# Graph attention over image windows: the neighbour sums run over all 128 rows, with a shifted copy of transposed x

## The reference, cut to what matters

```python
alpha = _bn_relu(einsum('bchw,oc->bohw', x, wa), ...)      # 32 channels, the queries
sigma = _bn_relu(einsum('bchw,oc->bohw', x, ws), ...)      # 32 channels, the keys
att = einsum('bkn,bkm->bnm', af, sf)
att = softmax(where(adj, att, NEG), axis=2)                # adj: the 8 neighbours of a pixel
h_s = einsum('bnm,bcm->bcn', att, xf)
Gc = einsum('bcn,bdn->bcd', xf, xf)
catt = softmax(where(cadj, Gc, NEG), axis=2)               # cadj: the channels c-1 and c+1
h_p = einsum('bcd,bdn->bcn', catt, xf)
out = (1.0 - gama) * x + gama * elu(h_s + h_p)
```

## Time and profile before

| what | value |
|---|---|
| median of 3 runs | 502.03 us (498.39 to 506.97) |
| the profiled execution, its own time | 500.11 us |
| its span | 498.0 us |
| mean granted TensorE clock | 0.982 |
| busy: TensorE, weight loads, ScalarE, VectorE, GpSimd | 93%, 70%, 69%, 68%, 59% |

### The profile page before, as it was taken

One profiled execution on the slowest core, in us unless ns is written; L12 is line 12 of the kernel. 1 busy time (PEld: TensorE's weight loads), 2 busy tenths in 40 slices (PEclk: granted clock), 3 DMA queues, 4 the chain that ended last, 5 costly groups with the idle time before them and its releaser, 6 DMA issues.

```text
span 498.0 us, 17890 instructions
## 1 busy us (share of the span) xinstructions
PE 461.8 (93%) x7172; PEld 350.4 (70%) x7172; DVE 339.3 (68%) x693; ACT 341.7 (69%) x980; POOL 295.2 (59%) x198
## 2 busy tenths in 40 slices
PE   1679999999999999999999999999999999999993
PEld 1346777768777786877767786877778687777783
DVE  6016676677767676766768677686767777686895
ACT  3336867677786777677776767787677776867571
POOL 8000566566756676567657656775666667665770
PEclk9998999999999999999999999999999999999985
DMA  7956667677776777676677767777677777644123
GB/s 224 264 137 166 190 206 241 194 217 225 224 226 211 236 209 239 206 238 210 206 228 215 243 203 226 222 228 224 217 218 231 219 224 226 197 156 143 65 107 128
DMA packets 55746, 102.01 MB, mean 205 GB/s; under 512 B 6256, under 2 KB 6640, under 8 KB 55664
## 3 DMA queue, kind: packets, MB, share of 16 engines
q1 hardware_dynamic: 55664, 100.88, 65.6%
HBM read 34.00 MB, written 33.55 MB: 136 GB/s over the span
## 4 chain that ended last, share of the span: by engine, by line
PE 84%; ACT 8%; DVE 3%; issue 3%; DMA 1%; SPq 0%; DVEq 0%; ACTq 0%
PE z L475 31%; PE gb L475 20%; PE xp L485 14%; PE score L475 12%; PE et L562 6%; ACT elu L302 2%; ACT key L263 2%; ACT upper L253 2%; PE gb L508 1%; ACT upper L267 1%; DVE elu L384 1%; DMA wt<-w_dram 1%; DVE z L379 1%; DVE probs_t L372 0%; DVE bn L424 0%
## 5 line engine op out<-in xcount | busy, mean ns | idle before, releaser
L228 POOL TENSOR_SCALAR elu<-elu,vec,mix 128x1024 f32<-128x1024 f32 x61 | 72.8, 1193 | 178.6 <-DVE elu L384 178.6
L475 PE MATMUL z<-probs_t,upper 64*128 64x128 f32 (+1 forms) x2304 | 173.2, 284 | 4.5 <-DVE probs_t L372 2.4
L475 PEld LDWEIGHTS z<-probs_t,upper 64*128 64x128 f32 x2304 | 155.2, 190 | 28.4 <-issue 24.1
L232 POOL TENSOR_TENSOR blend<-elu,blend 128x1024 f32<-128x1024 f32 x61 | 144.0, 2361 | 9.4 <-POOL elu L228 0.5
L302 ACT ACTIVATE elu<-z 128x512 f32<-128x512 f32 x128 | 69.7, 600 | 70.8 <-PE z L475 70.8
L384 DVE SCALAR_TENSOR_TENSOR elu<-elu,z 128x512 f32<-128x512 f32 x128 | 82.0, 682 | 35.4 <-ACT elu L302 35.4
L278 ACT ACTIVATE score<-score,neg_max 128x128 f32<-128x128 f32 x256 | 86.5, 338 | 25.1 <-DVE neg_max L355 25.1
L253 ACT ACTIVATE upper<-xp 128x512 f32<-128x512 f32 x128 | 76.8, 600 | 39.2 <-PE xp L485 39.2
L485 PE MATMUL xp<-const,x 128*128 128x128 f32 x512 | 87.2, 295 | 14.5 <-ACT upper L253 8.4
L379 DVE SCALAR_TENSOR_TENSOR z<-near,catt,z 128x512 f32<-128x512 f32 x128 | 90.4, 750 | 7.3 <-ACT z L293 6.6
L293 ACT ACTIVATE z<-x,catt 128x512 f32<-128x512 f32 x128 | 83.6, 695 | 2.4 <-DVE elu L384 2.4
(11 more groups left out here) (52 smaller groups left out, 244.1 us busy)
## 6 DMA issues: line engine op xcount, KB each, us to landing
x<-x_dram SPq DMA_DIRECT2D x64, 512.0 KB, 6.0
out_dram<-blend SPq DMA_DIRECT2D x61, 512.0 KB, 3.6
near<-x SPq DMA_DIRECT2D x128, 224.0 KB, 4.5
near<-x SPq DMA_DIRECT2D x128, 30.0 KB, 4.1
out_dram<-blend SPq DMA_DIRECT2D x6, 256.0 KB, 2.0
const<-constants_dram SPq DMA_DIRECT2D x1, 243.5 KB, 7.9
const<-constants_dram SPq DMA_DIRECT2D x1, 128.0 KB, 2.1
wt<-w_dram SPq DMA_DIRECT2D x1, 64.0 KB, 3.8
```

Source lines behind the costliest of these rows:

```text
L228: nc.gpsimd.tensor_scalar(elu[s % 2][:, :, :], elu[s % 2][:, :, :], vec[:, V_GAMA:V_GAMA + 1], mix[:, 1:2], ALU.mult, ALU.add).then_inc(ga ...
L232: nc.gpsimd.tensor_tensor(blend[s % BLENDS][:, :, :], elu[s % 2][:, :, :], blend[s % BLENDS][:, :, :], ALU.add).then_inc(blend_done, 1)
L475: return nc.tensor.matmul(o, l, r, start=start, stop=stop, skip_group_check=True, **kw)
```

## The change

The half-height products of z are replaced by products over all 128 partitions. A second copy of transposed x, `lower`, holds for each window v the lower half of group v on partitions 64 to 127 and the upper half of group v+1 on partitions 0 to 63. Two DMAs per step copy it from `upper`; the last group's upper half is written by ScalarE as before, now into `lower`. Then kind 0 of window v is one product with `upper[v]` and kind 1 is one with `lower[v]`, each of 64 columns. That is 4 windows by 2 kinds by 2 banks, 16 products for a step, in one phase.

With it go these edits. All z of step t-2 is summed once, near the end of the slot. `gram_band` part 2 moves behind the transposes of the probabilities, and part 3 behind z. `z_done` is raised once per bank, so `exp_z` of h waits for bank h alone. `near` shrinks from two whole images to five quarters, is built two slots ahead of its use in place of four, and is cleared by five smaller operations. The waits that named the old counts are rewritten.

```diff
-        near = [sb(f"near{j}", [P, HALF, N]) for j in range(2)]
-        upper = [sb(f"upper{j}", [P, GROUPS + 1, C]) for j in range(2)]
+        near = [sb(f"near{j}", [P, HALF, QN]) for j in range(NEAR_BUFS)]
+        upper = [sb(f"upper{j}", [P, GROUPS, C]) for j in range(2)]
+        lower = [sb(f"lower{j}", [P, GROUPS, C]) for j in range(2)]
...
-                    sp.wait_ge(near_in[(b - XBUFS) % 2][q], NEARS * ((b - XBUFS) // 2 + 1))
+                    sp.wait_ge(near_in[s % NEAR_BUFS], NEARS * (s // NEAR_BUFS + 1))
                 sp.dma_start(xs[b % XBUFS][:, :, cols(q)], x_img[b][:, :, q * QN:(q + 1) * QN])\
                     .then_inc(x_in[b % XBUFS][q], 16)
 
-            def build_near(b, q):
+            def build_near(s):
+                b, q = s // QUARTERS, s % QUARTERS
                 sp.wait_ge(x_in[b % XBUFS][q], 16 * (b // XBUFS + 1))
-                if b >= 2:
-                    sp.wait_ge(mix_done, 2 * ((b - 2) * QUARTERS + q) + 2)
-                j, signal = b % 2, near_in[b % 2][q]
+                if s >= NEAR_BUFS:
+                    sp.wait_ge(mix_done, 2 * (s - NEAR_BUFS) + 2)
+                to, signal = near[s % NEAR_BUFS], near_in[s % NEAR_BUFS]
                 xb = xs[b % XBUFS]
                 for lo, hi in ((0, SPREAD), (SPREAD, P - 1)):
-                    sp.dma_start(near[j][lo + 1:hi + 1, 0, q * QN:(q + 1) * QN], xb[lo:hi, 1, cols(q)]).then_inc(signal, 16)
-                    sp.dma_start(near[j][lo:hi, 1, q * QN:(q + 1) * QN], xb[lo + 1:hi + 1, 0, cols(q)]).then_inc(signal, 16)
+                    sp.dma_start(to[lo + 1:hi + 1, 0, :], xb[lo:hi, 1, cols(q)]).then_inc(signal, 16)
+                    sp.dma_start(to[lo:hi, 1, :], xb[lo + 1:hi + 1, 0, cols(q)]).then_inc(signal, 16)
+
+            def build_lower(s):
+                b, q = s // QUARTERS, s % QUARTERS
+                sp.wait_ge(xt_out, 2 * s + 2)
+                if b >= 2:
+                    sp.wait_ge(z_done, 2 * (s - 2 * QUARTERS) + 2)
+                j, g0 = b % 2, q * GQ
+                g1 = g0 + (q == 0)
+                sp.dma_start(lower[j][0:KEYS, g1 - 1:g0 + GQ - 1, :], upper[j][0:KEYS, g1:g0 + GQ, :])\
+                    .then_inc(lower_in[j][q], 16)
+                sp.dma_start(lower[j][KEYS:P, g0:g0 + GQ, :], upper[j][KEYS:P, g0:g0 + GQ, :])\
+                    .then_inc(lower_in[j][q], 16)
...
-            sp.wait_ge(near_zero, 2)
+            sp.wait_ge(near_zero, NEAR_BUFS)
             for t in slots:
                 b, q = t // QUARTERS, t % QUARTERS
+                if real(t + 3):
+                    build_lower(t + 3)
                 if b + 1 < B:
                     sp.wait_ge(xt_done, 2 * t + 2 * QUARTERS + 1)
                 if b + 2 < B:
                     load_x(b + 2, q)
-                if b + 1 < B:
-                    build_near(b + 1, q)
+                if real(t + 2):
+                    build_near(t + 2)
...
-                    act.wait_ge(z_done, (b - 1) * QUARTERS)
-                nc.scalar.activation(upper[b % 2][0:KEYS, GROUPS, :], gb[0:KEYS, EDGE:EDGE + C], ACT.Copy)\
+                    act.wait_ge(z_done, 2 * (b - 1) * QUARTERS)
+                nc.scalar.activation(lower[b % 2][0:KEYS, GROUPS - 1, :], gb[0:KEYS, EDGE:EDGE + C], ACT.Copy)\
...
-                act.wait_ge(z_done, s + 1)
+                act.wait_ge(z_done, 2 * s + h + 1)
...
-                    k = P if g < GROUPS else KEYS
+                    rows_t = upper[b % 2][:, g, :] if g < GROUPS else lower[b % 2][0:KEYS, GROUPS - 1, :]
                     for blk in range(P // HID):
                         mine, other = blk * HID, P + blk * HID - 1
-                        last = mm(gb[mine:mine + HID, 0:BAND], upper[b % 2][0:k, g, mine:mine + HID],
-                                  upper[b % 2][0:k, g, other:other + BAND], g == 0, g == GROUPS, tile_position=(0, mine))
+                        last = mm(gb[mine:mine + HID, 0:BAND], rows_t[:, mine:mine + HID], rows_t[:, other:other + BAND], g == 0, g == GROUPS,
+                                  tile_position=(0, mine))
...
-            def z_sums(s, phase):
-                b, q = s // QUARTERS, s % QUARTERS
-                if phase == 0:
-                    pe.wait_ge(pt_out, s + 1)
-                    pe.wait_ge(mix_done, 2 * s + 2)
-                else:
-                    pe.wait_ge(z_half, s + 1)
-                up, pt = upper[b % 2], probs_t[s % 2]
-
-                def add(row, h, g, lo, hi):
-                    return mm(z[s % 2][h][:, lo:hi], up[row:row + KEYS, GQ * q + g, h * P:(h + 1) * P],
-                              pt[row:row + KEYS, lo:hi], False, True, tile_position=(row, 0))
-
-                even, odd = phase, 1 - phase
-                add(0, even, 0, 0, KEYS)
-                for g in range(GQ):
-                    add(64, odd, g, g * WIN, (g + 1) * WIN)
-                    last = add(0, even, g + 1, g * WIN + KEYS, min((g + 1) * WIN + KEYS, QN))
-                last.then_inc(z_done if phase else z_half, 1)
+            def z_sums(s):
+                b, q = s // QUARTERS, s % QUARTERS
+                pe.wait_ge(pt_out, s + 1)
+                pe.wait_ge(mix_done, 2 * s + 2)
+                pe.wait_ge(lower_in[b % 2][q], 32 * (b // 2 + 1))
+                if q < QUARTERS - 1:
+                    pe.wait_ge(lower_in[b % 2][q + 1], 32 * (b // 2 + 1))
+                pt = probs_t[s % 2]
+                for h in range(HALF):
+                    for v in range(GQ):
+                        for c, rows_t in enumerate((upper[b % 2], lower[b % 2])):
+                            n0 = v * WIN + c * KEYS
+                            last = mm(z[s % 2][h][:, n0:n0 + KEYS], rows_t[:, GQ * q + v, h * P:(h + 1) * P],
+                                      pt[:, n0:n0 + KEYS], False, True)
+                    last.then_inc(z_done, 1)
...
-                if real(t - 2):
-                    z_sums(t - 2, 0)
-                if own:
-                    gram_band(b, 2)
                 if b + 1 < B:
                     transpose_x(b + 1, q, 1)
                 if real(t - 1):
                     transpose_probs(t - 1)
                 if own:
-                    gram_band(b, 3)
+                    gram_band(b, 2)
                 if q == 2 and 0 < b + 1 < B:
                     project_odd(b + 1)
                 if real(t - 2):
-                    z_sums(t - 2, 1)
+                    z_sums(t - 2)
+                if own:
+                    gram_band(b, 3)
                 if q == 1 and 0 < b + 1 < B:
                     project_query(b + 1)
                 if t == -1:
```

More of the change, by code:

```diff
@@ L29 @@
 NEARS = 4 * 16
+NEAR_BUFS = 5
 C_ID, C_DOWN = 0, P
@@ L104, in graph_attention @@
         x_in = [[sem(f"x_in{j}{q}") for q in range(QUARTERS)] for j in range(XBUFS)]
-        near_in = [[sem(f"near_in{j}{q}") for q in range(QUARTERS)] for j in range(2)]
+        near_in = [sem(f"near_in{j}") for j in range(NEAR_BUFS)]
+        lower_in = [[sem(f"lower_in{j}{q}") for q in range(QUARTERS)] for j in range(2)]
         stored = [sem(f"stored{i}") for i in range(BLENDS)]
@@ L138, in graph_attention @@
         mix_done = sem("mix_done")
-        z_half = sem("z_half")
         z_done = sem("z_done")
@@ L237, in _ @@
                 nc.gpsimd.memset(xs[j][:, :, W + N:N + 2 * W], 0.0).then_inc(pads_done, 1)
-            for j in range(2):
+            for j in range(NEAR_BUFS):
                 nc.gpsimd.memset(near[j][:, :, :], 0.0).then_inc(near_zero, 1)
@@ L251, in move_xt @@
                 if b >= 2:
-                    act.wait_ge(z_done, (b - 2) * QUARTERS + q + 1)
+                    act.wait_ge(z_done, 2 * ((b - 2) * QUARTERS + q) + 2)
                 nc.scalar.activation(upper[b % 2][:, g:g + 2, :], xp[:, :].rearrange("p (v c) -> p v c", v=2),
@@ L370, in move_probs @@
                 if s >= 2:
-                    dve.wait_ge(z_done, s - 1)
+                    dve.wait_ge(z_done, 2 * (s - 2) + 2)
                 nc.vector.tensor_copy(probs_t[s % 2][:, :], et[:, :]).then_inc(pt_out, 1)
@@ L375, in mix_channels @@
                 b, q = s // QUARTERS, s % QUARTERS
-                dve.wait_ge(near_in[b % 2][q], NEARS * (b // 2 + 1))
+                dve.wait_ge(near_in[s % NEAR_BUFS], NEARS * (s // NEAR_BUFS + 1))
                 dve.wait_ge(product_done, 2 * s + h + 1)
                 zh = z[s % 2][h]
-                nc.vector.scalar_tensor_tensor(zh[:, :], near[b % 2][:, h, q * QN:(q + 1) * QN], catt[:, h, h:h + 1],
+                nc.vector.scalar_tensor_tensor(zh[:, :], near[s % NEAR_BUFS][:, h, :], catt[:, h, h:h + 1],
                                                zh[:, :], ALU.mult, ALU.add).then_inc(mix_done, 1)
```

## The result

The kernel after takes 663.0 us in the median (654.6 to 663.9, 4 runs) against 504.5 us for the kernel before in the runs beside it: a ratio of 1.322, with a 95% interval of 1.302 to 1.342. The profiled execution spans 661.0 us, 163.0 more than before, and its mean granted TensorE clock is 0.833, where it was 0.982. I had forecast 578 us and a range of 560 to 612.

The account below looks back on a forecast made before the run. TensorE, busy for 93% of the span, was taken as the bound. Per image +4.20 + 0.10 + 0.95 - 0.40 = +4.85; sixteen images, less 0.95 for the first, give 76.7, plus 0.7 at the end, on 500.11: 578 us, range 560 to 612.

Parts of the forecast that it names:

- rival (a): TensorE's clock falls to 1.2 GHz at the open wait before the shift, 1.7 us each: 604 (0.10) or 686 us (0.09).
- my milder case: The clock falls about once per image, 1.7 us each, adding 27 us for 604 us in all; chance 0.10.
- the clock held through every image before: Argument against clock falls: in the trace before, the clock held in every image between first and last, 1.00 in one shown.
- z, four steps: z's 32 full-height loads set the pace at 0.111 us each: 3.55 us per step against 2.50, +4.20 per image.
- wait behind the band, scores included: Nothing hides VectorE's small operations ahead of the shift, and `normalise` delays the scores: +0.95 per image, between 0.8 and 1.2.
- wait in q 3: TensorE's 0.54 us wait for ScalarE before `project_even` shrinks as the first exponential starts earlier: -0.40 per image.
- seams: Costs where TensorE changes tile shape between groups, some vanishing, some dearer: +0.10 per image, between -0.2 and +0.4.
- another +0.7 for the half clock: At the end, the last z at half clock costs 2.3 more in place of 1.05, less 0.5 for the earlier exponential.
- Rival (b): In z, a full-height load waits for the matmul ahead: 0.166 us per product, 690 us in all; chance 0.05.
- Rival (c): z's full-height load is as short as a transpose's: 0.066 us per product, about 486 us, DMA engines nearly full; chance 0.07.
- The second part, the scores behind `normalise`: `normalise`, queued behind `gram_pick` on VectorE, releases the scores 1.70 us behind the band, TensorE being ready at 1.65.
- The copy, `near`, the queues: The two added transfers per step, the later `near` and the issues on SP's queue cost zero; waits on them are over when reached.

Follow-up runs that it names:

- run 3: Kernel after, with every product of z streaming 128 columns in place of 64 (sums not the reference's): 583.5 us, ratio 1.162.
- run 2: Kernel after, with four bfloat16 products of 512 columns, never read, put in the wait ahead of the shift: 571.4 us, ratio 1.135.
- run 5: Kernel before, with only TensorE's order changed to that of the kernel after, z keeping its half-height products: 554.6 us, ratio 1.090.
- Run 1: Kernel after, with part 3 of the band moved back in front of z: 572.1 us, ratio 1.129.
- run 4: Kernel after, with every product of z streaming 32 columns in place of 64, half the queries left out: 835.6 us, ratio 1.665.
- run 9: On top of run 2, same count of z's loads and matmuls, each over 64 rows, banks on the array's two halves, half the keys left out: 508.2 us.
- run 7: On top of run 2, the DMAs that build `lower` and the waits on them left out, both products reading `upper`: 571.3 us, ratio 1.128.
- run 8: Kernel after, with part 3 of the band back in front of z and every product of z streaming 128 columns: 553.5 us in two runs.

## Why the prediction was wrong

The step that failed is rival (a), the clock, in its price and in its chance. I priced a fall at 1.7 us, as if the clock came back after one stretch of 3.4 us as in the earlier trace rows, and gave falls about once per image 0.10 and about once per slot 0.09. The runs showed one fall in 12 of 15 intervals, nearly as often as my milder case, but 6.3 to 7.8 us dear in 11 of them, four times the price. For a fall of 3.4 us the price was right: those of run 3 cost 1.6. Twelve falls at 1.7 us would have come to 20 us and stayed inside my range; it is their length that I missed. In the first image of the kernel before, the projection of the queries came next, from 40.70, and the clock was back at 43.0. Here z at half clock came first, and z streams for at most half of the time even at full clock (an estimate: by run 3 a stream of 128 columns fits in the 0.11 us of a load). The argument "the clock held through every image before" spoke of a kernel without the open wait and with dense z. I had both changes in hand, each with its row, and did not join them.

What it cost: run 2, the kernel with the clock held, spans 568.7 us, so 92.3 of the 163.0 us are the clock's. Taking 33.25 us from each of the 14 intervals after the first leaves 75 us. The rest is nearly all the end: from the last shift on the kernel after takes 51.0 us, at clock 0.50 almost from its start, where run 2 and the kernel before take 32.8.

The other terms, per image at full clock:

| term | forecast | measured |
|---|---|---|
| z, four steps | +4.20 | 3.61 + 3.52 + 3.52 + 3.71 - 8 x 1.255 = +4.32 |
| wait behind the band, scores included (from run 5) | +0.95 | 0.94 + 0.19 = +1.13 |
| wait in q 3 | -0.40 | 0.20 - 0.54 = -0.34 |
| seams | +0.10 | what is left, -0.38 |
| image | 28.52 + 4.85 = 33.4 | 33.25 |

The four terms of z are the four steps in the first stretch of the busy-time table, 303.85 to 337.10. Run 1, which closes the wait behind the band in the kernel after itself, gave 1.34 in place of 1.13, so wait and seams are not cleanly parted, and the -0.38 is a remainder that no run explains.

The sum for a held clock, 577.5 us, stands against 570.6 for run 2's profiled execution, 1.2% less. Much of that is the end: I had each step's z dearer there and another +0.7 for the half clock, but run 2 takes as long from the last shift on as the kernel before (32.8 us), with 8.5 us at half clock where that has 14.7.

*z.* Right in mechanism and size. The load sets the pace at 0.11 us (runs 3 and 4), the matmul ahead is hidden beside it, and only half-height loads pair up (run 9). Rival (b), no overlap at full height, is refuted: by it 128 columns would have taken 0.22 us per product. The rule of the Trainium skill ("TensorE: Matmul & The Clock Gate", Part 3), by which a weight load overlaps a matmul in flight only when the row groups differ, does not describe these full-height products: 64 more columns in each of an image's 128 matmuls of z add 0.2 us to the image (run 3). Rival (c), the short load, is refuted as well: the load is like the shift's, not like the transposes'.

*The band.* Right, 0.87 us idle again. The second part, the scores behind `normalise`, I had at 0.1 and it is 0.19.

*The copy, `near`, the queues.* Right, at no cost per image: run 7 for the copy, and no wait of TensorE or VectorE on `lower` or `near` in the trace after. Rival (c)'s remark that the DMA engines would bound a much faster z is not shown: in run 9 they are 95% busy at 285 GB/s in an image of 27.47 us, but no wait of TensorE in that image is put down to a DMA.

What stays open: which property of the work the clock follows. The runs show that more columns beside the same loads bring fewer and shorter falls (runs 3, 4 and 8), that work in the wait takes them away (run 2), and that the share of time that the page calls busy does not tell, since TensorE was busy for all of 187.40 to 194.20 at half clock. Why the same open wait trips the clock in some intervals and not in others is open too; in the kernel after it comes in a fixed order, three intervals with a fall and one without. A gap in issue stands ahead of both long falls of run 1 and of all seven in run 9. That run 8 has such gaps and no fall agrees with a thin stream making them fatal, but they are few enough for chance, and no run made such a gap on purpose.

## What to carry to other kernels

A product of float32 with 128 weight columns costs its load if it streams few columns (128 and fewer here): count loads before columns, and see whether they lie side by side now. Before a wait is opened on TensorE, ask what comes behind it: if that is thin work, a fall of the clock is paid until the next dense work, 14 to 17 us here in place of 3.4. And when a small serial chain of another engine hangs between two TensorE groups, keep the big group between them; moving it out cost here 1.1 us per image directly and some five times that (75 us in 14 images) through the clock.

## What the runs showed of the hardware

The clock can stay at 1.2 GHz with TensorE nearly always busy: for 17 us at a time in the kernel after (16.6 of them busy, from 108.92 on), for 41 of 51 us per image in run 4. More streamed columns made a kernel faster: run 8 streams twice the columns of run 1 in z, and both of its runs took less time than all four of run 1. Work whose result nobody reads, four products of 512 columns per image in a gap, saved 92 us of span. Half-height loads of two halves of the array take 0.06 us each (1.93 us for 32), full-height ones 0.11. The DMA engines moved 285 GB/s over a whole image at a share of 0.95 (run 9); that this is their limit is not shown, since one stretch of 3.4 us in the kernel after has 302.
